# Last stage of a 12-stage decoder: the inverse root of the heads' norms on VectorE in eleven operations, in place of fourteen on GpSimd

## What is computed

```python
for i in range(6):
    x = attn_layer(shift_tokens(x), Wqkv[i], q_scale[i], k_scale[i], Wo[i]) + x
    x = ffn_layer(shift_tokens(x), ln_g[i], ln_b[i], W1[i], b1[i], W2[i], b2[i]) + x

# in attn_layer, 16 heads of 64:
l2norm = lambda t: t / max(norm(t, axis=-1), 1e-12)
q = l2norm(q) * q_scale;  k = l2norm(k) * k_scale
q = q * cos * scale + rotate_half(q) * sin * scale
k = k * cos / scale + rotate_half(k) * sin / scale
out = local_attention(q, k, v)      # windows of 32, keys of two windows
```

## Time and profile before

| | us |
|---|---|
| median of 3 runs | 2918.16 (2910.07 to 2920.03) |
| span of the profiled execution | 2892.0 |
| TensorE busy | 2565.0, 89% |
| VectorE busy | 1798.9, 62% |
| ScalarE busy | 1537.1, 53% |
| GpSimd busy | 1365.0, 47% |

### The profile page before, as it was taken

The page is one execution under the profiler, slowest core; times in us unless marked ns, Lnnn a source line. Parts: engine busy times, 40 slices in busy tenths (PEclk is TensorE's granted clock), DMA queues, the critical chain, the costliest instruction groups (busy, mean ns, idle before and its releaser), DMA issues. The chain is left out here.

```text
span 2892.0 us, 56780 instructions
## 1 busy us (share of the span) xinstructions
PE 2565.0 (89%) x20009; PEld 1646.1 (57%) x20009; DVE 1798.9 (62%) x4074; ACT 1537.1 (53%) x4979; POOL 1365.0 (47%) x1981
## 2 busy tenths in 40 slices
PE   6999978898989979866589997899999999999997
PEld 3555545555646646544345554566666666666665
DVE  4566655545657745555555555777677777777773
ACT  1455535524747736532245553566665666666654
POOL 0344434302536614300024444876776777767762
PEclk8899988999989999988799998999999999999998
DMA  2000000010000010000100001010101101011000
GB/s 69 1 1 1 1 8 2 12 33 5 2 4 2 2 33 1 6 1 8 28 1 1 1 1 58 12 38 20 31 23 31 34 20 30 27 27 34 20 25 7
DMA packets 45707, 47.77 MB, mean 17 GB/s; under 512 B 11947, under 2 KB 31414, under 8 KB 45431
## 3 DMA queue, kind: packets, MB, share of 16 engines
q1 hardware_dynamic: 45430, 44.18, 5.5%
HBM read 31.05 MB, written 0.52 MB: 11 GB/s over the span
## 5 line engine op out<-in xcount | busy, mean ns | idle before, releaser
L2264 ACT ACTIVATE net_probs<-bank,net_negmax 128x96 f32<-128x96 f32 x768 | 250.9, 338 | 191.4 <-DVE net_negmax L2397 191.2
L1033 DVE TENSOR_REDUCE negmax<-scores 128x1 f32<-128x508 f32 (+4 forms) x512 | 212.5, 467 | 211.2 <-PE scores L918 180.0
L1013 POOL TENSOR_TENSOR l_xattn_probs<-l_xattn_probs,rowinv 128x512 f32<-128x512 f32 x128 | 130.3, 1039 | 406.5 <-DVE rowinv L1025 406.5
L2326 POOL TENSOR_TENSOR net_probs<-net_probs,net_inverse 128x384 f32<-128x384 f32 x192 | 158.7, 826 | 237.8 <-DVE net_inverse L2393 237.8
L1013 POOL TENSOR_TENSOR lora_probs<-lora_probs,rowinv 128x508 f32<-128x508 f32 (+1 forms) x256 | 149.5, 617 | 246.2 <-DVE rowinv L1025 246.2
L2397 DVE TENSOR_REDUCE net_negmax<-bank 128x4 f32<-128x384 f32 x192 | 106.3, 554 | 242.9 <-PE bank L2099 242.3
L2318 POOL TENSOR_TENSOR net_rope<-net_rope,net_sin_parts 128x512 f32<-128x512 f32 x192 | 243.8, 1270 | 5.5 <-DVE net_sin_parts L2367 5.4
L124 DVE COPY turned<-flip 128x512 f32<-128x512 f32 (+3 forms) x280 | 163.0, 582 | 65.8 <-PE flip L945 52.9
L2336 POOL TENSOR_TENSOR net_rope<-net_rope,net_head_inv 128x512 f32<-128x512 f32 x192 | 201.2, 1048 | 0.0
L739 DVE TENSOR_REDUCE negmax<-scores 128x2 f32<-128x256 f32 (+2 forms) x192 | 157.6, 822 | 63.2 <-PE scores L647 35.5
L918 PE MATMUL scores<-kT,qM 64*128 64x512 f32 (+2 forms) x768 | 188.2, 567 | 8.3 <-ACT kT L122 4.8
(11 more groups left out here) (434 smaller groups left out, 6546.3 us busy)
## 6 DMA issues: line engine op xcount, KB each, us to landing
net_w_qkv<-in_L_ffn_Wqkv SPq DMA_DIRECT2D x12, 768.0 KB, 5.7
net_vals_between<-net_vals SPq DMA_DIRECT2D x48, 192.0 KB, 2.5
net_w_out<-in_L_ffn_Wo SPq DMA_DIRECT2D x6, 512.0 KB, 4.2
net_vals_between<-net_vals SPq DMA_DIRECT2D x48, 64.0 KB, 2.0
moe_w<-in_L_ffn_w13T SPq DMA_DIRECT2D x8, 256.0 KB, 2.7
net_w<-in_L_ffn_W SPq DMA_DIRECT2D x6, 341.0 KB
moe_w<-in_L_ffn_w2T SPq DMA_DIRECT2D x8, 128.0 KB, 2.4
ctx_tok<-in_ctx SPq DMA_DIRECT2D x1, 768.0 KB, 6.5
```

Source lines behind the costliest of these rows:

```text
L1013: last = nc.gpsimd.tensor_tensor(own, own, rowinv[:, u * tail + w:u * tail + w + 1].to_broadcast([P, k1 - k0]), ALU.mult)
L1033: last = nc.vector.tensor_reduce(negmax[:, u * tail + w:u * tail + w + 1], scores[:, 2 * qt + h, k0:k1], AX.X, ALU.max, negate=True)
L2264: last = nc.scalar.activation(prob_blocks(g)[:, w, :], score_blocks(g)[:, w, :], ACT.Exp, bias=maxima[:, g % 4, w:w + 1], accum_out=sums[: ...
L2326: nc.gpsimd.tensor_tensor(prob_blocks(g), prob_blocks(g), part, ALU.mult).then_inc(shared.sem, 1)
```

## The change

The root moves from GpSimd's queue to VectorE's. On GpSimd it stood behind the scaling and ahead of the addition; on VectorE it stands behind the sums of squares and ahead of the parts of the feed-forward network (`OUT`, `LATE` and on), in the same ticks (`PROJ + 5`). In each of the three improvements one operation `(t + 1.5) * y` takes the place of an addition and a product, which leaves 11. There are two waits ahead of it: for the sums of squares, and for GpSimd's scaling of the groups that used the same half of `head_inv` two roots ago.

```diff
-        ROOT_OPS, ROOT_MAGIC = 14, float(0x5F3759DF - (1 << 30) - (1 << 22))
+        ROOT_OPS, ROOT_MAGIC = 11, float(0x5F3759DF - (1 << 30) - (1 << 22))
...
-                    pool.wait_ge(step.sem, step.at(0, done[0]))
-            then(nc.gpsimd.tensor_scalar(half, src, floor, -0.5, ALU.max, ALU.mult))
-            then(nc.gpsimd.tensor_scalar(y.bitcast(I32), half.bitcast(I32), -0.5, ROOT_MAGIC, ALU.mult, ALU.add))
+                    dve.wait_ge(step.sem, step.at(0, done[0]))
+            then(nc.vector.tensor_scalar(half, src, floor, -0.5, ALU.max, ALU.mult))
+            then(nc.vector.tensor_scalar(y.bitcast(I32), half.bitcast(I32), -0.5, ROOT_MAGIC, ALU.mult, ALU.add))
             for r in range(3):
-                then(nc.gpsimd.tensor_tensor(t, y, y, ALU.mult))
-                then(nc.gpsimd.tensor_tensor(t, t, half, ALU.mult))
-                then(nc.gpsimd.tensor_scalar(t, t, 1.5, None, ALU.add))
-                then(nc.gpsimd.tensor_tensor(y if r < 2 else out, t, y, ALU.mult), last=(r == 2))
+                then(nc.vector.tensor_tensor(t, y, y, ALU.mult))
+                then(nc.vector.tensor_tensor(t, t, half, ALU.mult))
+                then(nc.vector.scalar_tensor_tensor(y if r < 2 else out, t, 1.5, y, ALU.add, ALU.mult), last=(r == 2))
...
-                        j = at_tick(s, PROJ + 5, 4, S // 2)
-                        if j is not None:
-                            pool.wait_ge(reduced.sem, reduced.at(0, 2 * j + 2))
-                            inverse_root(pool, head_sums[:, j % 2, :], 1e-24, head_inv[:, j % 2, :], head_temp, rooted, ROOT_OPS * j)
...
+                        j = at_tick(s, PROJ + 5, 4, S // 2)
+                        if j is not None:
+
+                            dve.wait_ge(reduced.sem, reduced.at(0, 2 * j + 2))
+                            until(dve, scaled, 4 * (j - 1))
+                            inverse_root(dve, head_sums[:, j % 2, :], 1e-24, head_inv[:, j % 2, :], head_temp, rooted, ROOT_OPS * j)
```

More of the change, by code:

```diff
@@ L1855, in decoder, with inverse_root @@
         by_batch = lambda v: v.rearrange("p (b n) -> p b n", b=B)
-        ROOT_OPS, ROOT_MAGIC = 14, float(0x5F3759DF - (1 << 30) - (1 << 22))
-        def inverse_root(pool, src, floor, out, temp, step, before):
+        ROOT_OPS, ROOT_MAGIC = 11, float(0x5F3759DF - (1 << 30) - (1 << 22))
+        def inverse_root(dve, src, floor, out, temp, step, before):
             half, y, t = temp[:, 0, :], temp[:, 1, :], temp[:, 2, :]
```

## The result

The changed kernel is slower: 2959.3 us median (2935.9 to 2961.2) against 2914.9 us (2910.1 to 2920.0) for the kernel before in the same series, four runs each; ratio 1.013, 95% interval 1.011 to 1.016. The forecast was 2947, range 2932 to 2968. The span of the profiled execution is 2955.9 us, and a run's time is only some 2 us more than its span (2957.69 for this one).

The account below looks back on a forecast made before the run. TensorE's work plus one wait per job was taken to bound the kernel. Tick 5 at 1.35 us times 22 (29.7), tick 1 at 0 and the ramp at -1 gave +29 on 2918.2: 2947 us, range 2932 to 2968.

Parts of the forecast that it names:

- What bounds the kernel: Last stage, steady state: TensorE's work plus one wait before L2086 per eight-tick job, 2.24 or 2.08 us.
- The price of the root: Eleven added VectorE operations take 2.4 us, bounds 2.06 and 2.8; in tick 5 all of it counts.
- The stall that goes: Tick 5: the layer norm's root, held by GpSimd's addition, falls from 3.45 to 2.33 us; 1.05 us saved in the mean.
- Tick 1 is free: Tick 1: the root fits VectorE's 2.03 us wait; L2187 waits about 0.25 us longer, the next wait shrinks as much; price 0.
- the 0.36 us hole: TensorE's wait before L2086 behind tick 1's root, from a ScalarE chain; expected to shrink to near 0.1 us.
- The ramp: Four roots before the first layer norm: between -8 and +6 us, taken as -1.
- the collisions: Rival: GpSimd's later additions hold VectorE's roots again, about 1.05 us in each of 44 ticks, near 2993 us; chance 0.10.
- The sum: Whole kernel: 29.7 us for tick 5, 0 for tick 1, -1 for the start of the stage, +29 us.
- the lower granted clock: Rival: TensorE stands still longer and its clock drops to 0.97 in all 22 jobs, 28 us more, near 2975; chance 0.03.
- The bound of 38.5 us: Upper bound for tick 5: 1.75 us net in each of 22 jobs, with a root of 2.8 us.
- the limit of 1.8: Sign of being wrong: jobs growing by over 1.8 us, meaning GpSimd holds VectorE or tick 1 costs time.
- Span and time: Profiled span 2892.0 us, median 2918.2, the 26 us between taken as lying around the span; span near 2921, time 2947 expected.

Follow-up runs that it names:

- the matmuls in the hole: Changed kernel with twelve matmuls of 128 x 512 bf16, whose result nobody reads, put on TensorE ahead of L2079 in tick 7; ratio to the kernel before 1.008.
- tick 5 alone: Against the kernel before, only the roots of tick 5 are made on VectorE, those of tick 1 stay on GpSimd; ratio 1.017.
- the longer root: Changed kernel with four improvements in place of three in every root, 14 operations on VectorE; 3000.2 us in one run.
- tick 1 alone: Against the kernel before, only the roots of tick 1 are made on VectorE, those of tick 5 stay on GpSimd; 2913.5 against 2914.8 us, ratio 1.000.
- the root behind the addition: Kernel before with GpSimd's root queued behind the addition of the same tick instead of ahead of it; 2890.8 against 2914.8 us, ratio 0.991.

## Why the prediction was right, point by point

- *What bounds the kernel.* Right: TensorE, with one hole a job that goes with VectorE one for one. Taking 24 of the 48 roots off GpSimd in tick 1 changed nothing, so the page's chain of a quarter of the span on GpSimd was no bound.
- *The price of the root.* 2.34 us against 2.4; the step from the widths of 2 and 64 columns was good to 3%.
- *The stall that goes.* Right: the layer norm's root takes 2.33 us in every job. Net 1.28 us a job against 1.35.
- *Tick 1 is free.* Right, and with more room than I read. The wait at L2180 grew by 0.04 us, not by 0.25, and the one behind it shrank by 0.03. The term that was off is the distance from the root to L2406: I had taken 2.4 us for the root and 0.7 us from the reciprocal to L2406, and these are 2.34 and 0.53. So the 0.36 us hole, which I wanted to see near 0.1, is still 0.33.

VectorE and TensorE of the changed kernel, tick 1, answering to the earlier trace rows:

```profile
2190.75 0.17 DVE L1869 TENSOR_SCALAR net_head_temp<-net_head_sums 128x32 f32<-128x32 f32 x1
...
2193.09 0.17 DVE L2382 RECIPROCAL net_inverse<-net_sums 128x4 f32<-128x4 f32 x1
2193.17 0.53 DVE L2386 TENSOR_REDUCE net_negmax<-bank 128x4 f32<-128x384 f32 x1
2193.62 0.47 DVE L2395 SCALAR_TENSOR_TENSOR net_acts<-bank,net_layer_cols,net_gelu 85x256 f32<-85x256 f32 x1
...
2194.14 1.13 PE L2180 MATMUL bank<-net_znT,net_w 128*128 128x256 f32 x4 [0.22 <-DVE net_acts L2395]
```

- *The ramp.* From the stage's first projection to the first layer norm's root it is 86.2 us, 87.7 before: -1.5 against my -1, gain and price meeting as described. One operation of VectorE's root took 1.19 us there, beside an addition of 1.26 us on GpSimd, and in two further roots of the ramp one took 0.60: the collisions that I had as a rival exist, but none falls between the first hole and the last. The Trainium skill (SBUF — State Buffer, Who interferes with whom) states that a VectorE instruction in a 2-port mode and GpSimd block each other for the whole instruction; the 1.19 us of this `tensor_scalar` agree. In steady state GpSimd waits during both roots, so the rule decides nothing.

```profile
1829.54 1.26 POOL L2311 TENSOR_TENSOR net_rope<-net_rope,net_sin_parts 128x512 f32<-128x512 f32 x1
1829.65 1.19 DVE L1870 TENSOR_SCALAR net_head_temp<-net_head_temp 128x32 int32<-128x32 int32 x1
```

- *The sum.* +29 forecast; the measured ratio of 1.013 is +39, the medians differ by 44. The terms that the sum had, root, stall and ramp, were right: they came to 26.9 - 2.5 = 24 us in the traces. The step that failed is in the rivals: I gave the lower granted clock a chance of 0.03, as a case of its own with 28 us, reasoning from one stretch of 100 us that shows 0.97. It should have been a term of the sum. The stretch at 2.24 us of hole already had two such jobs, and the change makes the hole half as long again. It came to 21 us in the trace, nearly as much as all the other terms, and the matmuls in the hole showed that the hole is its cause. That the range held the time was luck in this: its upper end stood for a root of 2.8 us, for less room in tick 1 and for a dearer ramp, none of which came. The bound of 38.5 us behind it was also some 2 us too high, since 2.8 us does not take off the 0.12 us behind the last operation that the lower bound takes off. One of my own signs of being wrong did show: in the mean the jobs grew by 47.9 / 21 = 2.28 us, over the limit of 1.8, at the full clock by 1.28. The causes that I had named for it, collisions and tick 1, are not the ones; the lower clock is.
- *Span and time.* I took the 26 us between the span of the profiled execution and the median for work around the span. It is 2 us (2914.82 for a span of 2912.6 in a later run of the same kernel); the profiled execution was simply a quick one. As I added a difference to the median, nothing in the forecast hung on it, but my span of 2921 was wrong for that reason.

What stays open: why one hole of 3.42 us in three is spared the lower clock, and how many jobs had it in the unprofiled runs. The run of 2935.9 us among four of about 2960 had a mean granted clock of 0.944 where the others had 0.931 to 0.933, so it may have been spared most of it; no trace of it exists.

## What to carry to other kernels

In a hand-ordered pipeline ask of a step not which engine has time for it, but between which two events of the bound engine's loop it will stand: the same 2.34 us cost 1.28 us net a job in tick 5 and nothing in tick 1, and in tick 4 they were hidden and left a gain of 1.04 us. When an operation in a chain of small ones takes seven times its usual time, look at what ends with it on another engine (here GpSimd's addition): reordering that engine's queue may give nearly the whole gain with nothing moved. And before counting a new wait of TensorE once, look in the trace for what its clock did behind the waits that are there already.

## What the runs showed of the hardware

- Behind holes of 3.42 us TensorE's granted clock fell to 0.50 for about three microseconds in 15 of 21 periods (14 of 21 with tick 5 alone, 21 of 21 with the longer root, which has a further wait of 0.52 us ahead), at 1.56 us each in nearly all; behind holes of 2.24, 2.09 or 2.08 us in 2 of 21 (in the kernel before and with tick 1 alone); behind 1.12, 1.18 and 0.84 us in none.
- In these chains a VectorE operation on 128 x 32 float32 that waits for the one before starts 0.226 us after its start; one that doesn't wait, here z's copy, starts after 0.11 us (2171.22 to 2171.33). On 128 x 2 it is 0.196 and 0.08 us.
- With the root behind the addition, where short GpSimd operations of 0.25 to 0.29 us run beside most of it, the layer norm's root lost 0.06 us in all. In the kernel before it lost up to 1.12 us: one operation took 1.19 instead of 0.16 beside the addition of 1.27 us, and the one ahead of it 0.27 instead of 0.17 us.
